# Counting edges by one-hots: a group's eight pair rows from one comparison, the edge weights moved to the place rows

## The reference

```
deg = max(segment_sum(1, dst), 1);  dis = deg ** -0.5
h = relu(layernorm(x))                       # layer 0: ten hops
for r in layer_reg:                          # e = dis[dst] * dis[src]
    agg  = segment_sum(feat[src] * e, dst)
    feat = r * (0.9 * agg + 0.1 * h) + (1 - r) * feat
x = x + feat
h = relu(layernorm(x))                       # layer 1: four GRU steps, 4 edge types
m = (emb @ W_msg.T + b_msg).reshape(n, 4, 128)
r = segment_sum(m[src, type], dst);  emb = gru(r, emb)
out = x + emb
```

## Time and profile before

| | us |
|---|---|
| median of the 3 runs | 2555.01 (2551.72 to 2556.26) |
| the profiled execution, own time | 2550.86 |
| its span, first to last instruction | 2549.3 |
| TensorE / VectorE / ScalarE / GpSimd busy | 2190.8 / 1488.7 / 335.0 / 134.9 |
| mean granted TensorE clock | 0.921 |

### The profile page before, as it was taken

The page is one execution under the profiler, slowest core; times in us unless marked ns, Lnnn a source line. Parts: engine busy times, 40 slices in busy tenths (PEclk is TensorE's granted clock), DMA queues, the critical chain, the costliest instruction groups (busy, mean ns, idle before and its releaser), DMA issues.

```text
span 2549.3 us, 41289 instructions
## 1 busy us (share of the span) xinstructions
PE 2190.8 (86%) x14375; PEld 1440.7 (57%) x14886; DVE 1488.7 (58%) x3473; ACT 335.0 (13%) x494; POOL 134.9 (5%) x391
## 2 busy tenths in 40 slices
PE   1544545559999999999799999999999999999996
PEld 1322333348999898988644455444554446544464
DVE  6988999977777777777662234522444324442243
ACT  0322223330000000000121011210112100220000
POOL 1322222200000000000000000000000000000000
PEclk9996555559999999999899999999999999999998
DMA  2000000010000000001400000000000000000001
GB/s 72 21 21 21 21 21 21 28 41 2 1 2 2 2 2 2 1 2 49 139 1 1 1 1 1 1 1 1 1 1 1 1 1 1 1 1 1 1 1 50
DMA packets 22188, 34.32 MB, mean 13 GB/s; under 512 B 2450, under 2 KB 18442, under 8 KB 21469
## 3 DMA queue, kind: packets, MB, share of 16 engines
q1 hardware_dynamic: 19025, 30.56, 3.5%
q10 hardware_dynamic: 2944, 0.93, 0.2%
HBM read 18.04 MB, written 13.45 MB: 12 GB/s over the span
## 4 chain that ended last, share of the span: by engine, by line
PE 75%; DVE 15%; issue 5%; DVEq 2%; DMA 2%; ACT 0%; POOLq 0%; ACTq 0%; POOL 0%
PE ps L787 41%; PE ps L706 26%; DVE hot_pair L967 8%; PE ps L739 3%; PE ps L727 2%; DVEq L961 2%; DVE dig L990 1%; DVE hot_place L964 1%; DVE big L993 1%; DMA big<-in_L_gnn_w_hh 1%; PE ps L647 1%; DMA x_after_hops<-x 1%; PE ps L691 1%; PE ps L605 1%; DVE dig L992 1%
## 5 line engine op out<-in xcount | busy, mean ns | idle before, releaser
L787 PE MATMUL ps<-slots,m_parts 125*128 125x500 fp8e4 (+1 forms) x5600 | 1088.0, 354 | 6.6 <-DVE m_parts L1337 5.2
L787 PEld LDWEIGHTS ps<-slots,m_parts 125*128 125x128 f16 x5600 | 547.4, 98 | 495.7 <-issue 10.0
L706 PE MATMUL ps<-parts,big 125*128 125x256 f16 x6125 | 669.6, 273 | 6.8 <-issue 4.2
L706 PEld LDWEIGHTS ps<-parts,big 125*128 125x128 fp8e4 x6125 | 591.3, 98 | 63.6
L605 PE MATMUL ps<-hot_pair,hot_place 125*128 125x228 f16 x1000 | 230.6, 400 | 256.5 <-DVE hot_pair L967 256.5
L1255 DVE TENSOR_SCALAR slots<-big 128x3200 int32<-128x3200 int32 (+1 forms) x112 | 244.1, 2183 | 279.8 <-PE ps L787 279.7
L605 PEld LDWEIGHTS ps<-hot_pair,hot_place 125*128 125x128 f16 x1000 | 143.1, 149 | 343.8 <-DVE hot_pair L967 283.1
L967 DVE TENSOR_SCALAR hot_pair<-iota_pair,win 125x228 f16<-125x228 f16 x1000 | 262.5, 334 | 3.1 <-issue 3.1
L1357 DVE SCALAR_TENSOR_TENSOR r_parts<-ps,over,r_parts 128x500 f16<-128x500 f32 (+1 forms) x28 | 19.1, 684 | 230.1 <-ACT r_parts L527 230.1
L1364 DVE SCALAR_TENSOR_TENSOR gate_r<-ps,over,gate_r 128x500 f32<-128x500 f32 (+1 forms) x28 | 19.1, 682 | 229.3 <-PE ps L739 221.8
L1183 DVE SCALAR_TENSOR_TENSOR hop_tmp<-ps,coef,g 125x128 f32<-125x128 f32 x250 | 87.6, 350 | 97.9 <-PE ps L706 94.4
(11 more groups left out here) (200 smaller groups left out, 1130.2 us busy)
## 6 DMA issues: line engine op xcount, KB each, us to landing
packed_counts<-packed SPq DMA_DIRECT2D x16, 625.0 KB, 3.3
big<-packed_counts SPq DMA_DIRECT2D x4, 1600.0 KB, 7.3
big<-packed_counts SPq DMA_DIRECT2D x3, 1200.0 KB, 6.5
hd<-in_x SPq DMA_DIRECT2D x1, 1562.5 KB
x_again<-in_x SPq DMA_DIRECT2D x1, 1562.5 KB
x_after_hops<-x SPq DMA_DIRECT2D x1, 1562.5 KB
big<-x_after_hops SPq DMA_DIRECT2D x1, 1562.5 KB
out<-big SPq DMA_DIRECT2D x4, 250.0 KB
```

Of the source, the lines that this page charges most:

```text
L706: last = pe.matmul(ps[:, n % RING, 0:2 * F], tot_f8[0:Q, c, a, :], both((parts0, parts1)[par], a), start=a == 0, stop=a == TILES - 1)
L787: last = pe.matmul(ps[:, k % 2, 0:SIZES[k] * Q], m_parts[0:Q, a, h, t * F:(t + 1) * F], slots_f8[0:Q, t % 2, 0:SIZES[k], a, 0:Q], start=a ...
```

## The change

- The pair rows carry no weight any more. One comparison over 8 x 228 elements (`iota_pair` repeated eight times against the key of each chunk, held for 228 elements) makes them, stored chunk after chunk.
- The weight goes to the place rows. VectorE marks the places of chunks 0 to 5 (`marks`) and of chunks 6 and 7 (`marks_d`) in two comparisons. ScalarE copies each of the six with the weight of the edge as its scale into `weighed` (contiguous rows of 128); VectorE multiplies the two others into `weighed_d`.
- All of these have four buffers in place of two (DEPTH), and GpSimd's window has too: one copy of places and weights in 16 bit, one of the weights in 32 bit, and the subtraction, which now writes 16 bit. The offset of a group in the keys is 456 for 1024, so that near keys are exact in 16 bit.
- TensorE waits for the pairs once a group, for `weighed` chunk by chunk, and gives one increment a group.
- ScalarE takes out a group two groups late, and parts the lanes one by one behind the groups 3, 4 and 5 of the next block.
- The digits of a block are summed ahead of the last group of the next, and by five instructions in place of six.

```diff
+            def stage_window(q, b):
+                lo = pool.value_load(windows[0:1, ds(q, 1)], min_val=0, max_val=NCH)
+                pool.wait_ge(s_hot_used, q + 1)
+                pool.tensor_copy(win_pw[0:CH, b, :, :], tab[0:CH, :, ds(lo, W)])
+                pool.tensor_copy(win_w[0:CH, b, :], tab[0:CH, 1, ds(lo, W)])
+                pool.tensor_tensor(win_key[0:CH, b, :], keys[0:CH, ds(lo, W)], q_off[0:CH, ds(q, 1)].broadcast_to([CH, W]),
+                                   ALU.subtract).then_inc(s_wst, 1)
...
+            def weigh(q, b):
+                act.wait_ge(s_marks, q + 1)
+                for w in range(WA):
+                    act.activation(weighed[0:CH, b, w, :], marks[0:CH, b, :, w], ACT.Copy,
+                                   scale=win_w[0:CH, b, w:w + 1]).then_inc(s_weighed, 1)
+
+            def block_of(turn, b, n, turn_before):
                 blk = 2 * turn + b
-                act.wait_ge(s_bytes, blk + 1)
                 for j in range(n):
-                    evacuate(blk, b, j)
-                part_lanes(blk, turn, b, BQ * blk + n - 1)
-
+                    weigh(BQ * blk + j, j % DEPTH)
+                    if j >= 2:
+                        evacuate(blk, b, j - 2)
+                    elif turn_before is not None:
+                        evacuate(2 * turn_before + 1 - b, 1 - b, BQ - 2 + j)
+                    if 3 <= j < 3 + LANES and turn_before is not None:
+                        part_lane(turn_before, 1 - b, j - 3, 16 * turn_before + BQ * (1 - b) + BQ - 1)
...
                 pe.wait_ge(s_taken, q + 1)
+                pe.wait_ge(s_pairs, q + 1)
                 for w in range(W):
-                    pe.wait_ge(s_hot, W * q + w + 2 * W + 1)
-                    pe.matmul(ps[:, j, 0:KP], hot_place[0:CH, b, :, w], hot_pair[0:CH, b, w, :],
-                              start=w == 0, stop=w == W - 1, skip_group_check=True).then_inc(s_hot_used, 1)
+                    if w < WA:
+                        pe.wait_ge(s_weighed, WA * q + w + 1)
+                    elif w == WA:
+                        pe.wait_ge(s_weighed_d, q + 1)
+                    place = weighed[0:CH, b, w, :] if w < WA else weighed_d[0:CH, b, :, w - WA]
+                    last = pe.matmul(ps[:, j, 0:KP], place, hot_pair[0:CH, b, w, :],
+                                     start=w == 0, stop=w == W - 1, skip_group_check=True)
+                last.then_inc(s_hot_used, 1)
...
-                dve.wait_ge(s_hot_used, W * q + W)
-                TT(hot_place[0:CH, b, :, :], iota_place[0:CH, :, :],
-                   win_p[0:CH, b:b + 1, :].broadcast_to([CH, 128, W]), ALU.is_equal)
-                for w in range(W):
-                    TS(hot_pair[0:CH, b, w, :], iota_pair[0:CH, :], win[0:CH, b, 0, w:w + 1],
-                       win[0:CH, b, 1, w:w + 1], ALU.is_equal, ALU.mult).then_inc(s_hot, 1)
+                dve.wait_ge(s_hot_used, q + 1)
+                TT(marks[0:CH, b, :, :], iota_place[0:CH, :, 0:WA],
+                   win_pw[0:CH, b, 0:1, 0:WA].broadcast_to([CH, 128, WA]), ALU.is_equal).then_inc(s_marks, 1)
+                TT(marks_d[0:CH, b, :, :], iota_place[0:CH, :, WA:W],
+                   win_pw[0:CH, b, 0:1, WA:W].broadcast_to([CH, 128, WD]), ALU.is_equal).then_inc(s_marks_d, 1)
+                TT(hot_pair[0:CH, b, :, :], iota_pair[0:CH, :].rearrange("p (o n) -> p o n", o=1).broadcast_to([CH, W, KP]),
+                   win_key[0:CH, b, :].rearrange("p (w o) -> p w o", o=1).broadcast_to([CH, W, KP]),
+                   ALU.is_equal).then_inc(s_pairs, 1)
+                dve.wait_ge(s_marks_d, q + 1)
+                TT(weighed_d[0:CH, b, :, :], marks_d[0:CH, b, :, :],
+                   win_pw[0:CH, b, 1:2, WA:W].broadcast_to([CH, 128, WD]), ALU.mult).then_inc(s_weighed_d, 1)
...
-                step(TT(u16[0], u16[0], u16[1], ALU.add))
-                TS(high, low, NIBBLES, None, ALU.bitwise_and)
-                step(TS(lower, low, 4, NIBBLES, ALU.logical_shift_right, ALU.bitwise_and))
-                step(TT(big1[:, :].bitcast(DT.uint16).rearrange("p (n q) -> p n q", q=64)[:, :, ds(4 * blk, 4)],
-                        u16[1].rearrange("p (n q) -> p n q", q=4), u16[2].rearrange("p (n q) -> p n q", q=4), ALU.add))
+                step(TT(low16, low16, high16, ALU.add))
+                step(TS(high16, low16, 1.0 + 1.0 / 16, None, ALU.mult))
+                step(TS(big1[:, :].bitcast(I32).rearrange("p (n q) -> p n q", q=32)[:, :, ds(2 * blk, 2)],
+                        high.rearrange("p (n q) -> p n q", q=2), NIBBLES, None, ALU.bitwise_and))
                 dve.sem_inc(s_digits, 1)
...
-            HEAD = BQ // 2
-            for j in range(HEAD):
-                onehots(j, j % 2)
+            for j in range(BQ):
+                onehots(j, j % DEPTH)
             with dve.Fori(0, NB // 2 - 1) as i:
                 steps.loop(i, 8)
                 for b in range(2):
                     for j in range(BQ):
-                        onehots(2 * BQ * i + BQ * b + HEAD + j, j % 2)
-                    sum_digits(2 * i + b, b)
+                        onehots(2 * BQ * i + BQ * (b + 1) + j, j % DEPTH)
+                        if j == BQ - 2:
+                            sum_digits(2 * i + b, b)
             steps.done(NB // 2 - 1)
```

More of the change, by code:

```diff
@@ L51 @@
 KP = 228
-KQ = 1024
+KQ = 456
+KG = 1024
+NOWHERE = -4096.0
 BQ = 8
@@ L58 @@
 BANKS = 8
+DEPTH = 4
+WA = 6
+WD = W - WA
 class Chain:
@@ L366, in stage @@
                 pool.tensor_copy(win_p[0:CH, b, :], tab[0:CH, 0, ds(lo, W)]).then_inc(staged, 1)
-            with pool.Fori(0, Q // 2) as i:
-                stage(2 * i, 2 * i, 0, s_hot, s_wst)
-                stage(2 * i + 1, 2 * i + 1, 1, s_hot, s_wst)
-            stage(Q - 1, Q - 1, 0, s_hot, s_wst)
+            def stage_window(q, b):
[5 more added lines that the diff above has]
+                                   ALU.subtract).then_inc(s_wst, 1)
+            with pool.Fori(0, Q // DEPTH) as i:
+                for j in range(DEPTH):
+                    stage_window(DEPTH * i + j, j)
+            for q in range(Q // DEPTH * DEPTH, Q):
+                stage_window(q, q % DEPTH)
             def share_largest():
@@ L458, in evacuate @@
                 q = BQ * blk + j
[L459 removed]
+                act.wait_ge(s_hot_used, q + 1 + DEPTH)
                 summed(q, extras, s_more_used)
+                if j == 0:
+                    act.wait_ge(s_bytes, blk + 1)
                 act.activation(words[:, b, :, j], ps[:, j, 0:KP], ACT.Copy, scale=float(ONE)).then_inc(s_taken, 1)
[L463 to L472 removed]
@@ L474, in block_of, with part_lane @@
-            def block_of(turn, b, n):
+            def part_lane(turn, b, l, last):
+                blk = 2 * turn + b
+                if l == 0:
+                    act.wait_ge(s_taken, last + 1 + BANKS)
+                    act.wait_ge(s_digits, blk + 1)
+                    act.wait_ge(s_packed[b], 16 * turn + 16)
+                lanes = words[:, b, :, :].bitcast(U8).rearrange("p n (q l) -> p (n q) l", l=4)
+                n = min(LANE, TILES - l * LANE) * TILES * BQ
+                at = l * LANE * TILES * BQ
+                ins = act.activation(packed[:, b, at:at + n], lanes[:, 0:n, l], ACT.Copy)
+                if l == LANES - 1:
+                    ins.then_inc(s_bytes, 1)
@@ L486, in _ @@
+            evacuate(NB - 1, 1, 4)
+            for l in range(LANES):
+                part_lane(NB // 2 - 1, 1, l, Q - 1)
             root(1)
@@ L639, in _ @@
                 for j in range(BQ):
[L640 removed]
+                    count(BQ * i + j, j % DEPTH, j)
             for j in range(Q - (NB - 1) * BQ):
[L642 removed]
+                count(BQ * (NB - 1) + j, j % DEPTH, j)
             pe.wait_ge(s_digits, NB + 2)
@@ L1104, in _ @@
                 step_g(TS(tab_e[width, 1, :], tab_e[width, 0, :], 3, None, ALU.logical_shift_right))
+                step_g(TS(tab_f[width, :], keys[width, :], 1.0 / KQ, MAGIC, ALU.mult, ALU.add))
+                step_g(TS(tab_f[width, :], tab_f[width, :], -MAGIC, None, ALU.add))
+                step_g(STT(out=keys[width, :], in0=tab_f[width, :], scalar=float(KG - KQ), in1=keys[width, :],
+                           op0=ALU.mult, op1=ALU.add))
                 step_g(STT(out=keys[width, :], in0=tab_e[width, 1, :], scalar=float(LANE * TILES), in1=keys[width, :],
```

57 lines of the change are left out of this document (28 added, 29 removed).

## The result

The changed kernel takes 2587.90 us (median of 4 runs, 2585.43 to 2589.28) against 2554.86 of the kernel before (a fourth run of it beside the three in the table ahead): a ratio of 1.0133, 95% interval 1.012 to 1.0147, 33 us slower. The forecast was 2581 us with a range from 2535 to 2650, and 0.70 for slower.

What follows compares the result with a forecast made beforehand. VectorE's stream, its idle time included, was taken to bound the counting stage. Terms 41 - 19 - 7 + 7 + 4 = +26 us on the profiled 2550.86 gave 2577, or 2581 us against the runs' median; range 2535 to 2650.

Steps and rivals of the forecast that it cites:

- Pair rows: VectorE's eight scalar instructions, 2.01 us a group, become one comparison of 1824 elements, bounds 1.02 and 1.97 us, taken 1.97.
- the prediction's law: VectorE's two-byte tensor-tensors with advancing inputs: 0.526 ns an element and 145 ns fixed.
- Place rows: VectorE's place comparison split in two plus a multiply; with short runs and pair rows +0.33 us a group, +41 us.
- Digit sums: VectorE's last three digit instructions become a multiply and a masked store: 5.0 us each sum, -19 us (-24 to -2).
- Loop edge: VectorE's idle at the loop's edge now follows a group: 1.0 us less in each of 7 turns, -7 us.
- ScalarE: Six scaled copies a group hide on average; digit sums wait 0.5 us a block for lanes, +7 us (0 to 30).
- third rival: ScalarE becomes the pace-maker at 0.42 us a copy; each block waits 2 us and more: +50, 2605 us; chance 0.10.
- End of the stage: Block 14's digit sums, now behind the last group, wait about 4 us for the third lane: +4 us (0 to 6).
- GpSimd: Its three small operations a group stay hidden, costing nothing, with four ends of VectorE instructions a group to get in.
- first rival: GpSimd starved by VectorE's two-input instructions; VectorE idles some 0.4 us a group: +50, 2631 us; chance 0.12.
- second rival: Long pair comparison runs at two a cycle, 1.02 us; ScalarE sets the pace: about -75, 2480 us; chance 0.13.

Runs made afterwards that it cites:

- e1: Changed kernel with the pairs stored chunk innermost, so keys advance along the inner dimension and TensorE reads in 16-byte steps: 2562.76 us, ratio 1.0029.
- e8: Changed kernel with the pairs stored as four blocks of 228 x 2, so the key advances over two chunks and TensorE steps 4 bytes: 2556.15 us, ratio 1.0001.
- e4: Kernel before with only the new five-instruction digit sums, at their old place: 2541.12 us, ratio 0.9948.
- e6: Changed kernel with four chunks weighted by ScalarE in place of six (WA = 4): 2578.61 us, ratio 1.009.
- e7: Changed kernel with two buffers in place of four (DEPTH = 2): 2604.52 us, ratio 1.0191.
- e9: e8 with four chunks weighted by ScalarE in place of six (WA = 4): 2489.43 us, ratio 0.9746.
- e2: Changed kernel with the one long pair comparison undone into eight scalar comparisons without the weight, which also use 4-byte keys: 2571.05 us, ratio 1.0063.
- e5: Changed kernel with a block's digits summed three groups later, behind the second group of the block after next: 2571.63 us, ratio 1.0061.
- e10: e9 with the digits summed three groups later, as in e5: 2466.11 us, ratio 0.965.

## Why the prediction was right

The sign, the cause and most sizes held; the time was 7 us above the forecast. Part of that closeness is luck: the forecast added 26 us, the medians rose by 33 and the profiled execution by 38, and one term was wrong by 10 us. By its own steps:

*Pair rows.* Taken at 1.97 us by the only row with a held value, L1267; measured 2046 ns, 1.97 from start to start. The decisive choice between bounds of 1.02 and 1.97 was right. L1267 was a row of 4 bytes and left open whether width or the held value made it slow; e1 and e8 settle it, with 1097 and 1096 ns at the same width and size. The Trainium skill's rule ("Vector Engine (DVE) Microarchitecture Reference", section 5.1), one result a cycle where one element is read again and again, agrees with these numbers: 2046 less the 145 of the prediction's law is 1.04 ns an element.

*Place rows.* 0.47 + 0.20 + 0.20 by the law, and 0.10 for short runs. Measured 0.47 + 0.29 + 0.20, 0.96 for 0.97. The third that was taken stands, but all of it falls on the comparison of 256 with runs of 4 bytes (371 ns for 280); runs of 12 bytes cost nothing (551 ns for 549). Group 2.93 for 2.94: 125 x 0.32 = **+40** for +41.

*Digit sums.* This is the term that was mis-sized. Taken at 5.0 us, measured 5.49 (302.09 to 307.58) and 5.87 in alternate blocks, where 0.54 us of idle stand ahead of the last instruction (273.17 in the turn before) in place of 0.15. The multiply was at the low bound (812 ns), the strided store at the high one: 1456 ns for 1250 words, whereas L1044 takes 804 for as many contiguous ones. Before, the sums took 6.2 us on average; the 6.24 that the prediction read is the longest of the sixteen. Over 16 sums that is **-8.8** (14 x 0.53 and twice 0.7), for -19. e4, without the idle time, has -11.4. Why that idle time comes in one surrounding (the changed kernel, e1, e6, e7, e8, e9) and not in the other (e2, e4, e5, e10) is open.

*Loop edge.* The idle behind the sums stayed at 1.01, the edge fell from 2.9 to between 1.80 and 2.00 us: 3.9 us a turn in place of 4.95, **-7** as forecast. The trace puts it down to TensorE's `ps`. Against that, e6, with four matmuls a group waiting for ScalarE in place of six and a longer group, has nearly the same (1.7 to 1.9); in the changed kernel, e6, e8 and e10 the group at the edge takes 4.7 to 5.1 us to the start of the next whatever its own length (2.93, 2.98, 2.0, 2.03). It looks like a fixed time, of which a shorter group uncovers more; that is argued, not shown. In e2 it is 7.1 to 7.3, with eleven instructions in the group; why was not tried.

*ScalarE.* A copy takes 0.36 us from start to start (six in 2.24 us, the last of them 0.45), 0.07 more than the contiguous 0.29, where 0.42 had been the bound. That bound was itself a slip: with the 280 ns that it takes off L507 (387 less 107), L461's 602 ns for 228 elements are 1.4 ns an element and not 1.8, and a copy would come to 0.37. The forecast took a wait of 0.5 us a block; measured 10.9 us in 14 blocks (15.5 less 4.6), 0.78 each: **+11** for +7. The third rival's wait of 2 us and more did not come.

*End of the stage.* "About 4 us" for the third lane, measured 4.58: **+4.6** for +4.

*GpSimd.* Costed at nothing; it costs eleven late windows, 0.17 us each, **+1.9** in all. The first rival's picture is right in kind, and e7 shows its size once the slack of four buffers is gone. The prediction's comfort, four ends of instructions a group for three operations, did not hold, since ends are missed (three in a row at 315.24); the four groups of lead did. The Trainium skill ("SBUF — State Buffer", "Who interferes with whom") says that a two-input instruction of VectorE keeps GpSimd's read waiting until its end; here the trace agrees, 2.98 us for an operation of 0.2, through several such instructions in a row.

*Sum.* 40 - 8.8 - 7 + 11 + 4.6 + 1.9 = +41.7, against +39.1 seen in the stage. The forecast's sum had left 0.5 us a turn unexplained in the kernel before (59.2 for 59.7), and counted nothing for it:

```profile
254.64 1.84 DVE L967 TENSOR_SCALAR hot_pair<-iota_pair,win 125x228 f16<-125x228 f16 x7 [0.46 <-issue]
```

This idle time behind the first pair row at the loop's edge is 3.1 us in the whole stage before, and none stands ahead of the pair comparison now. With it the sum is 38.6. The 2.0 us that were gained behind the stage are within what the kernel before differs from itself, and need no cause.

*The second rival* was wrong for this layout and right that ScalarE would then matter most: with the fast comparison ScalarE's work fills most of a turn. It put that case at 2480 us, and e8 has 2556. It added up ScalarE's work alone, 47 us a turn; that work is 49.2 in e8, but 11.7 us of waiting for marks come on top. The two engines' times don't hide each other: VectorE waits at the digits for ScalarE (93 us), then ScalarE for VectorE. Its 2480 is only approached with two copies moved to VectorE as well (e9, 2489).

## What to carry to other kernels

Merging eight narrow instructions into a wide one pays only if the wide one keeps the rate: see whether each operand advances along the inner dimension, and if one does not, store the result so that two do, and see what that stride does to the reader (here TensorE, whose matmuls came 0.18 us apart at 4 bytes and 0.40 at 16). Then place the work for the engine that the faster stream uncovers: of 119 us gained on VectorE 32 came through, and 90 more only when ScalarE's share was cut and the step that waits for it moved back. A high busy share does not yet name that engine: TensorE at 51 of 60 us cost 7 us, ScalarE at 48 was in the ring that set the turn. Small operations on GpSimd beside a stream of two-input instructions want enough buffers to miss some ends of instructions: with four they cost 1.9 us here, with two 34.
